# Attention output turned by VectorE in 32x32 blocks, self terms turned through DRAM, the tanh input taken from x W1 plus attention times (Wo W1), the loop written out

## The chip, the core and the metric

One core of a Trainium2 chip runs the program. The metric is the device time of one execution in microseconds. TensorE (PE) does the matrix products and can turn 128x128 tiles, VectorE (DVE), ScalarE (ACT) and GpSimd (POOL) work elementwise, and SyncE (SP) issues the transfers between DRAM and the on-chip memory. Each engine takes its instructions in order and waits on semaphores.

## The reference, cut to what matters

For 8 batches, x and side are 256 rows by 256 columns. There are 16 heads of 16 columns.

```python
# layer 0: attention of side's rows over x's keys and one own key ("self")
q = (side + b_self) @ Wq + bq
k_prev, k_self = (x + b_prev) @ Wk + bk, (side + b_self) @ Wk + bk
v_prev, v_self = x @ Wv + bv, side @ Wv + bv
score = concat([mask(q k_prev^T), sum(q * k_self)]) / 4      # per head
w = softmax(score)
attn = w[..., :-1] @ v_prev + w[..., -1:] * v_self
x1 = x + attn @ Wo + bo
# layer 1: pooling under a mask chosen by an integer per batch
s = tanh(x1 @ W1 + b1) @ v
out = x1 + softmax(masked(s)) @ x1 / count
```

## The kernel before

**Periods and slots.** The work is a pipeline over periods, numbered -1 to 9 here (`i` and `k` in the code: period 2i+k). In period n three or four batches are on the way: `nxt` is batch n+1 (its inputs are turned and q, k, v made), `b` is batch n (its score maxima are found), `prv` is batch n-1 (exponentials, product with v, normalization), `old` is batch n-2 (product with Wo, layer 1, output). Each period of TensorE has eight slots; each slot begins with one head pair's scores for the maximum (L1037) and one pair's scores for the exponential (L1050), which lags six slots, and then holds a piece of the other work. All periods are written in one function per engine; on the compute engines periods 3 to 6 run in a hardware loop of two periods per turn, the others are written out (SP's loop holds periods 2 to 5).

**Precision.** fp32 operands of large products are split into a rounded `hi` and a rest `lo`, and three products are summed: twelve TensorE instructions for a 256x256x256 product (L1010).

**Maxima.** VectorE reduces the scores of each pair (L798). There is one PSUM tile for these scores, so a slot's max scores wait for the maximum of the slot before. After four pairs the negated maxima are turned on TensorE (L1071; in slot 5 for the first half, in slot 0 of the next period for the second), copied by ScalarE and sent by SP into two rows of the q operand (L323), from which the exp scores take them.

**Attention output.** With v in 32-column groups, TensorE makes the output of four heads at a time with columns on partitions (L1063), ScalarE copies it to SBUF (`o_sb`, L519), TensorE turns it back (L1233, eight turns per batch, slot 7), VectorE adds the self term and its weight (L959, L963), GpSimd multiplies with the reciprocal sum (L469). In the next period TensorE turns `attn` again (L1142), ScalarE and VectorE split it into `at_hi` and `at_lo` (L567, L850), and TensorE makes the product with Wo (slot 2). VectorE adds `x_bo`, that is x plus the output bias, and so has x1. TensorE turns x1 (L1168), the two engines split that, and Z = x1 W1 follows in slot 4 with six products (L1188), then the tanh, then the product that spreads the score row over all partitions (L1202, tile SB).

**SP's queue.** In each period SP issues, in this order: loads of x and side two batches ahead, the second half's maxima, the spills of q and k parts to DRAM for the next batch (L305), the first half's maxima, the placing of the next batch's rows from DRAM (L314 and the mask L353, first half, then second half), and the load of `xr_sb`, x again in rows for the residual (L362). It waits for each piece's producers in this order.

**GpSimd's order.** The self product `vs_p` of `prv`, `q_lo`, the rest of x1 (L458), `attn` of `prv`, `x_bo` of `prv` (L479, waits for the load of `xr_sb`), then the issue of the output store of `old` (L484).

**Shared PSUM.** Four PSUM banks are handed from step to step by the table `SHARED`, whose entries name the bank and the reader that frees it.

## Time and profile before

| | us |
|---|---|
| median of three runs | 287.01 (286.06 to 287.28) |
| the profiled execution | 285.36, its span 283.7 |
| TensorE busy | 235.7 (83%) |
| VectorE busy | 174.6 (62%) |
| ScalarE busy | 150.1 (53%) |
| GpSimd busy | 65.6 (23%) |

The mean granted clock of TensorE was 0.937. A row of the timeline gives the start in us from the span's start, the duration, the engine, the source line, the operation with output and inputs, how many instructions are merged, and in brackets the idle time before it with what ended it. Rows of the windows view give the busy time of each engine in a stretch. TensorE's instructions overlap one another, so distances between starts say more than durations.

### The profile page before, as it was taken

Reading aid. Unit: us, or ns where it says so; the run is one execution under the profiler, and the core shown is the slowest. Engines: PE = TensorE matmul, PEld = TensorE weight load, DVE = VectorE, ACT = ScalarE, POOL = GpSimd, SP = SyncE. Lnnn points to the kernel's source line nnn. Section 1 sums busy time; section 2 is a strip of 40 time slices with the busy share of each in tenths; the row PEclk is TensorE's granted clock in tenths of the full one; section 3 lists DMA queues with packets and bytes.
Section 4 is the critical chain, followed back from the end, with each engine's and each line's share of the span. In section 5 each row is a group of like instructions: output and inputs, shape, how many; then the busy total and the mean of one; then the engine's idle time right before and its main releaser. Section 6 shows DMA issues by size and latency. Waiting matters only on the chain.

```text
span 283.7 us, 6002 instructions
## 1 busy us (share of the span) xinstructions
PE 235.7 (83%) x2084; PEld 186.7 (66%) x2084; DVE 174.6 (62%) x367; ACT 150.1 (53%) x289; POOL 65.6 (23%) x80
## 2 busy tenths in 40 slices
PE   2967598898899999999999999999998868666543
PEld 1866476677678777877887888688875636435422
DVE  2636665457568678758774978297748756324231
ACT  4341314474586657656865685468565656650220
POOL 8060010030151016101700270045005203404101
PEclk9999979599999999999999999799999999999555
DMA  6359866733964394359445943754375110201001
GB/s 151 101 191 246 162 210 160 158 112 117 206 154 166 101 206 165 130 137 228 143 138 127 211 152 111 172 94 148 111 170 101 37 39 1 77 0 39 0 0 37
DMA packets 28277, 35.50 MB, mean 125 GB/s; under 512 B 4440, under 2 KB 24672, under 8 KB 28256
## 3 DMA queue, kind: packets, MB, share of 16 engines
q1 hardware_dynamic: 27616, 33.12, 45.7%
q0 software_dynamic: 640, 2.10, 2.1%
q8 instruction: 13, 0.21, 0.3%
q14 instruction: 8, 0.07, 0.1%
HBM read 20.26 MB, written 14.69 MB: 123 GB/s over the span
## 4 chain that ended last, share of the span: by engine, by line
PE 57%; DMA 13%; DVE 11%; issue 9%; ACT 5%; SPq 3%; DVEq 0%; POOL 0%; ACTq 0%
PE ps_any L1010 20%; PE ps_any L1063 9%; DMA q_rows<-mt_sb 7%; PE ps_max L1037 7%; PE ps_any L1017 6%; PE ps_exp L1050 5%; DVE s_max L798 4%; DMA k_rows<-k_spill 3%; SPq L323 2%; PE ps_any L1188 2%; PE ps_any L1120 2%; PE ps_any L1233 2%; DMA x_sb<-in_x 2%; DVE o_out L983 1%; PE ps_max L1082 1%
## 5 line engine op out<-in xcount | busy, mean ns | idle before, releaser
L798 DVE TENSOR_REDUCE s_max<-ps_max 128x4 f32<-128x1024 f32 x64 | 78.0, 1219 | 26.0 <-PE ps_max L1037 25.7
L512 ACT ACTIVATE pt<-ps_exp 128x1024 f32<-128x1024 f32 x64 | 65.7, 1027 | 33.8 <-PE ps_exp L1050 33.5
L1037 PE MATMUL ps_max<-k_rows,q_rows 49*128 49x256 f32 x256 | 33.1, 338 | 9.5 <-DVE s_max L798 4.9
L469 POOL TENSOR_TENSOR attn<-num,rden 128x256 f32<-128x256 f32 x16 | 9.6, 621 | 124.4 <-DVE rden L968 124.4
L1063 PE MATMUL ps_any<-pt,v_aug 128*32 128x256 f32 x512 | 36.0, 401 | 1.3 <-DVE masked L924 1.3
L1037 PEld LDWEIGHTS ps_max<-k_rows,q_rows 49*128 49x128 f32 x256 | 19.8, 190 | 25.6 <-issue 13.8
L1050 PE MATMUL ps_exp<-q_rows,k_rows 51*128 51x256 f32 x256 | 27.9, 296 | 9.3 <-DMA q_rows<-mt_sb 8.3
L1050 PEld LDWEIGHTS ps_exp<-q_rows,k_rows 51*128 51x128 f32 x256 | 20.2, 190 | 13.3 <-DMA q_rows<-mt_sb 10.4
L1063 PEld LDWEIGHTS ps_any<-pt,v_aug 128*32 128x32 f32 x512 | 13.7, 112 | 12.8 <-issue 3.6
L1010 PE MATMUL ps_any<-st_hi,w_hi 128*128 128x256 f32 x64 | 20.7, 323 | 0.2 <-DVE st_lo L826 0.2
L1010 PE MATMUL ps_any<-st_hi,w_lo 128*128 128x256 f32 x64 | 19.1, 298 | 0.0
L1010 PE MATMUL ps_any<-st_lo,w_hi 128*128 128x256 f32 x64 | 19.1, 298 | 0.0
L942 DVE TENSOR_TENSOR pool_pt_lo<-ps_any,pool_pt_hi 128x512 fp32r<-128x512 f32 x8 | 5.5, 692 | 21.8 <-ACT pool_pt_hi L650 21.8
L434 POOL TENSOR_TENSOR q_lo<-q_full,q_hi 128x512 fp32r<-128x512 f32 x8 | 10.3, 1282 | 27.4 <-ACT q_hi L683 26.1
L519 ACT ACTIVATE o_sb<-ps_any 128x256 f32<-128x256 f32 x32 | 12.1, 379 | 7.9 <-PE ps_any L1063 7.7
L446 POOL TENSOR_TENSOR vs_p<-v_self,p_self 128x256 f32<-128x256 f32 x16 | 9.6, 620 | 23.6 <-ACT p_self L576 23.5
L1010 PEld LDWEIGHTS ps_any<-st_hi,w_hi 128*128 128x128 f32 x64 | 13.4, 209 | 1.6 <-DVE st_lo L826 0.6
L458 POOL TENSOR_TENSOR x_lo<-x,x_hi 128x512 fp32r<-128x512 f32 x8 | 10.2, 1274 | 15.5 <-ACT x_hi L585 15.5
L1010 PEld LDWEIGHTS ps_any<-st_hi,w_lo 128*128 128x128 f32 x64 | 13.3, 208 | 0.0
L895 DVE SCALAR_TENSOR_TENSOR k_lo<-ps_any,bqk_col,k_hi 128x256 fp32r<-128x256 f32 x16 | 7.0, 480 | 10.0 <-ACT k_hi L601 10.0
L1010 PEld LDWEIGHTS ps_any<-st_lo,w_hi 128*128 128x128 f32 x64 | 13.2, 206 | 0.0
L1010 PE MATMUL ps_any<-xt_hi,w_hi 128*128 128x256 f32 x32 | 10.7, 335 | 2.5 <-ACT q_hi L683 2.5
(141 smaller groups left out, 568.8 us busy)
## 6 DMA issues: line engine op xcount, KB each, us to landing
q_rows<-q_spill SPq DMA_DIRECT2D x32, 192.0 KB, 4.4
k_rows<-k_spill SPq DMA_DIRECT2D x32, 192.0 KB
q_spill<-q_hi SPq DMA_DIRECT2D x16, 256.0 KB, 2.5
k_spill<-k_hi SPq DMA_DIRECT2D x16, 256.0 KB, 2.5
s_sb<-in_fside_BxSxS SPq DMA_DIRECT2D x8, 256.0 KB, 6.1
x_sb<-in_x SPq DMA_DIRECT2D x8, 256.0 KB, 5.8
q_spill<-q_lo SPq DMA_DIRECT2D x8, 256.0 KB, 2.3
k_spill<-k_lo SPq DMA_DIRECT2D x8, 256.0 KB, 2.7
```

The source lines that it names most:

```text
L434: nc.gpsimd.tensor_tensor(lo[:], full[:], hi[:].bitcast(F32), ALU.subtract).then_inc(lo_done, 1)
L446: last = nc.gpsimd.tensor_tensor(vs_p[:, t].rearrange("p (h d) -> p h d", d=DH), v_self[:, par, t].rearrange("p (h d) -> p h d", d=DH), p_ ...
L458: nc.gpsimd.tensor_tensor(x1_lo[:], x1[:], x1_hi[:].bitcast(F32), ALU.subtract).then_inc(x1_lo_done, 1)
L469: nc.gpsimd.tensor_tensor(attn[:, t].rearrange("p (h d) -> p h d", d=DH), num[:, t].rearrange("p (h d) -> p h d", d=DH), rden[:, t].unsque ...
L512: nc.scalar.activation(pt[:, at:at + 2], ps_exp[:], ACT.Exp).then_inc(p_ready, 1)
L519: nc.scalar.activation(o_sb[:, g], ps_any[:, bank_free(f"PV{g}", i, k)[0], 0, :], ACT.Copy).then_inc(pv_copied, 1)
L798: nc.vector.tensor_reduce(s_max[:, j // MJ, :, j % MJ], ps_max[:], AX.X, ALU.max).then_inc(max_found, 1)
L1010: last = pe.matmul(out_of[:, m], lhs, rhs, start=(j == 0), stop=(j == len(terms) - 1))
L1017: last = pe.transpose(out_of[:, kb, P * t:P * t + P], src[:, t, P * kb:P * kb + P], ident[:])
L1037: last = pe.matmul(ps_max[:, e, t], q_rows[par][rows, j, P * t:P * t + P], k_rows[par][rows, j, :], start=True, stop=True)
L1050: last = pe.matmul(ps_exp[:, e, t], k_rows[par][rows, j, P * t:P * t + P], q_rows[par][rows, j, :], start=True, stop=True)
L1063: last = pe.matmul(bank[32 * c:32 * c + 32, 0, :], v_aug[par][:, t, h, :], pt[:, h % 8, t, :], start=(t == 0), stop=(t == KB - 1), skip_gr ...
```

## The change

1. **Attention output.** v's columns are put in another head order (by the way Wv is split), and four heads out of every fourth group share a step, so that VectorE can turn a PSUM bank of 128 x 512 in 32x32 blocks straight into rows (`turn`, twice per batch: after slot 3's maxima and after slot 7's). GpSimd adds the self terms (two instructions of 272 elements per partition) and multiplies with the reciprocals (two of 256), VectorE turns the result back with two 128x256 turns into `at_full`, ScalarE makes `at_hi` at the end of the period, and GpSimd makes `at_lo` as its first work of the next period. The `o_sb` copies, TensorE's turns of `o_sb` and `attn` and their PSUM banks go.
2. **Self terms.** GpSimd writes the weighted self values and their weights to `self_nat`; SP stores that to DRAM after the spills and loads it back in four transfers (`self_turned`, 128 x 544 bytes each) between the first half's maxima and the placing of the next batch's rows.
3. **tanh input.** Z is made from x turned (four buffers kept) times W1 plus attn turned times (Wo W1): twelve products in slot 3 instead of six in slot 4; x1 is no longer turned or split that way. (Wo W1) and its bias are made once in period 0. SB moves from slot 5 to slot 4.
4. **Head order of the score rows** (`slot_of`), with Wq and Wk split in two or four instructions where there were one or two, and the bias loads of q and k issued as eight transfers by ScalarE at the start instead of two by SP.
5. **Loop.** All eleven periods are written out on every engine.

```diff
 @@ sync, period @@
                 if live(*nxt):
                     spill(*nxt, (q_hi, q_lo), q_copied, q_lo_done, (0, 0, 1), q_spill, q_placed, 32, q_spilled)
                     spill(*nxt, (k_hi, k_lo), k_hi_done, k_lo_done, (0, 1, 0), k_spill, k_placed, 48, k_spilled)
+                if live(*prv):
+                    sp.wait_ge(vs_p_done, count(*prv, 1, 1))
+                    sp.dma_start(self_dram, self_nat[:].rearrange("p (c g) t d -> p c (g t d)", c=4)
+                                 ).then_inc(self_stored, 16)
                 if live(*b):
                     place_max(*b, 0)
+                if live(*prv):
+                    if (n := count(*prv, 2, 0)) is not None:
+                        sp.wait_ge(sum_done, n)
+                    sp.wait_ge(self_stored, count(*prv, 16, 16))
+                    for c in range(4):
+                        sp.dma_start(self_turned[32 * c:32 * c + 32].rearrange("p w n d -> p w (n d)"),
+                                     self_dram.rearrange("(w i) c m -> c i w m", i=32)[c]
+                                     ).then_inc(self_placed, 16)
 @@ gpsimd, period @@
+                if live(*old):
+                    pool.wait_ge(at_hi_done, count(*old, 1, 1))
...
+                    nc.gpsimd.tensor_tensor(at_lo[:], at_full[:], at_hi[:].bitcast(F32), ALU.subtract
+                                            ).then_inc(at_lo_done, 1)
                 if live(*prv):
...
-                    for t in range(KB):
-                        last = nc.gpsimd.tensor_tensor(
...
+                    nc.gpsimd.tensor_tensor(
+                        self_nat[:, :, :, 0:DH],
+                        v_self[:, par].rearrange("p t (n d) -> p n t d", d=DH),
+                        self_nat[:, :, :, DH:DH + 1].broadcast_to([P, H, KB, DH]), ALU.mult
+                        ).then_inc(vs_p_done, 1)
...
                 if live(*prv):
-                    pool.wait_ge(rden_done, count(*prv, 1, 1))
-                    for t in range(KB):
-                        pool.wait_ge(num_done, count(*prv, 2, t + 1))
-                        nc.gpsimd.tensor_tensor(
-                            attn[:, t].rearrange("p (h d) -> p h d", d=DH),
...
+                    pool.wait_ge(self_placed, count(*prv, 64, 64))
+                    for a in range(2):
+                        half = slice(NG * a, NG * a + NG)
+                        pool.wait_ge(o_turned_done, count(*prv, 2, a + 1))
+                        nc.gpsimd.tensor_tensor(
+                            o_turned[:, half, :, 0:DH + 1], o_turned[:, half, :, 0:DH + 1],
+                            self_turned[:].rearrange("p w n d -> p n w d")[:, half], ALU.add).then_inc(sum_done, 1)
...
+                    for a in range(2):
+                        pool.wait_ge(rden_done, count(*prv, 2, a + 1))
+                        nc.gpsimd.tensor_tensor(
+                            attn[:, a].rearrange("p n b d -> p b n d"),
...
+                                ).broadcast_to([P, 2, 8, DH]), ALU.mult).then_inc(attn_done, 1)
 
                     pool.wait_ge(xr_loaded, count(*prv, 16, 16))
 @@ scalar, period @@
-            def pv_copy(i, k, g):
...
-                nc.scalar.activation(o_sb[:, g], ps_any[:, bank_free(f"PV{g}", i, k)[0], 0, :], ACT.Copy).then_inc(pv_copied, 1)
                 exp_slot(3)
                 if live(*old):
-                    act.wait_ge(x1t_ready, count(*old, 1, 1))
-                    nc.scalar.activation(x1t_hi[:], ps_any[:, bank_free("X1T", i, k)[0]], ACT.Copy
-                                         ).then_inc(x1t_hi_done, 1)
+                    act.wait_ge(z_ready, count(*old, 1, 1))
...
+                    nc.scalar.activation(z_sb[0:A], ps_any[0:A, bank_free("Z", i, k)[0], 0, :], ACT.Tanh,
+                                         bias=b1_full[:, 0:1]).then_inc(tanh_done, 1)
...
                 exp_slot(7)
                 if live(*nxt):
...
+                if live(*prv):
+                    act.wait_ge(at_full_done, count(*prv, 2, 2))
...
+                    nc.scalar.activation(at_hi[:], at_full[:], ACT.Copy).then_inc(at_hi_done, 1)
...
+                for n, vec in enumerate((bq, bk)):
+                    for e, odd in ((0, 0), (0, 1), (1, 0), (1, 1)):
+                        act.dma_start(bqk_raw[odd::2, n, e:e + 1], vec.rearrange("(m e b d) -> e b d m", e=2, b=2, d=DH)[e, odd]
+                                      ).then_inc(bias_loaded, 16)
             weight_hi(0)
 @@ vector @@
+            def turn(i, k, a, pi, pk):
+                dve.wait_ge(pv_ready, count(i, k, NG, 2 * a + 2))
...
+                nc.vector.transpose(o_turned[:, NG * a:NG * a + NG].rearrange("p n w d -> p (n w d)"),
+                                    ps_any[:, bank_free("PVAB"[0:2] + "AB"[a], pi, pk)[0]].rearrange("p b q -> p (b q)")
+                                    ).then_inc(o_turned_done, 1)
...
                 if live(*b):
                     max_of(*b, 3)
                     group_max(*b, 0)
+                if live(*prv):
+                    turn(*prv, 0, i, k)
...
                     max_of(*b, 7)
                     group_max(*b, 1)
                 if live(*prv):
-                    natural = [ps_any[:, bank_free(f"NAT{t}", i, k)[0]].rearrange("p t (h c) -> p (t h) c", c=32)
-                               for t in range(KB)]
...
+                    turn(*prv, 1, i, k)
+                    for a in range(2):
+                        dve.wait_ge(sum_done, count(*prv, 2, a + 1))
+                        nc.vector.reciprocal(rden[:, half], o_turned[:, half, :, DH]).then_inc(rden_done, 1)
+                    for a in range(2):
+                        dve.wait_ge(attn_done, count(*prv, 2, a + 1))
+                        nc.vector.transpose(at_full[:, a], attn[:, a].rearrange("p n b d -> p (n b d)")
+                                            ).then_inc(at_full_done, 1)
...
+                if (i, k) == (0, 0):
+                    dve.wait_ge(w1o_ready, 1)
+                    nc.vector.tensor_copy(w1o_hi[:], ps_any[:, 3, :, 0:A]).then_inc(w1o_hi_done, 1)
+                    nc.vector.tensor_tensor(bias_col[:], ps_any[:, 3, :, A], bo_col[:], ALU.add
+                                            ).then_inc(bias_col_done, 1)
...
                 if live(*b):
                     max_of(*b, 5)
 @@ tensor, period @@
                 score_slot(3)
-                if live(*old):
-                    bank = take_bank("X1T", i, k)
-                    pe.wait_ge(x1_done, count(*old, 1, 1))
-                    transposed(bank, x1).then_inc(x1t_ready, 1)
                 if live(*nxt):
-                    products(bank, xt_hi, xt_lo, 1, True).then_inc(k_ready, 1)
+                    products(bank, *xt, 1, True).then_inc(k_ready, 1)
                 if live(*old):
                     bank = take_bank("Z", i, k)
-                             for w, x in ((w1_hi, x1t_hi), (w1_lo, x1t_hi), (w1_hi, x1t_lo))]
+                    terms = [(kb, w, x) for (w_a, w_b), (x_a, x_b) in (((w1_hi, w1_lo), old_xt),
+                                                                     ((w1o_hi, w1o_lo), (at_hi, at_lo)))
+                             for kb in range(KB) for w, x in ((w_a, x_a), (w_b, x_a), (w_a, x_b))]
+                if (i, k) == (0, 0):
+                    pe.wait_ge(wo_turned_done, 1)
...
+                                pe.matmul(ps_any[:, 3, kb, 0:A], wo_turned[:, nb, P * kb:P * kb + P], w1[:, nb, :],
+                                          start=(nb == 0), stop=(nb == KB - 1))
...
+                                last = pe.matmul(ps_any[:, 3, m, A:A + 1], w_raw[:, 3, kb, P * m:P * m + P],
+                                                 bv_col[:, kb:kb + 1], start=(kb == 0), stop=(kb == KB - 1))
 
                 score_slot(4)
...
+                if live(*old):
+                    bank = take_bank("SB", i, k)
+                    pe.wait_ge(tanh_done, count(*old, 1, 1))
                 score_slot(6)
-                    products(v_bank, xt_hi, xt_lo, 2, False, (0,))
...
                 score_slot(7)
                 if live(*nxt):
-                    products(v_bank, xt_hi, xt_lo, 2, False, (1,)).then_inc(v_ready, 1)
...
-                        for gg in range(NG):
-                            last = pe.transpose(bank[:, gg // 2, P * (gg % 2):P * (gg % 2) + P],
-                                                o_sb[:, gg, P * t:P * t + P], ident[:])
+                    products(bank, *xt, 2, False).then_inc(v_ready, 1)
```

## Rows read from the trace of the kernel before

**Rows 1.** Windows, period 4: us, busy us (instructions) PE PEld DVE ACT POOL, PEclk, DMA share, GB/s
```profile
131.70:158.79 27.09, 26.33 (x260) 21.37 (x259) 20.25 (x42) 17.91 (x35) 6.95 (x8) 1.00 0.59 154
```

**Rows 2.** Timeline of TensorE, single lines: start us, us, engine, line, operation, count, idle before
```profile
66.83 0.28 PE L1071 MATMUL ps_any<-ident,neg_max 128*32 128x128 f32 x1
...
148.04 0.28 PE L1071 MATMUL ps_any<-ident,neg_max 128*32 128x128 f32 x1
...
151.99 0.50 PE L1050 MATMUL ps_exp<-q_rows,k_rows 51*128 51x256 f32 x4 [0.57 <-DMA q_rows<-mt_sb]
...
158.79 0.51 PE L1037 MATMUL ps_max<-k_rows,q_rows 49*128 49x256 f32 x4
...
161.20 0.50 PE L1037 MATMUL ps_max<-k_rows,q_rows 49*128 49x256 f32 x4
...
164.98 0.39 PE L1010 MATMUL ps_any<-w_hi,at_hi 128*128 128x256 f32 x1
...
174.93 0.28 PE L1071 MATMUL ps_any<-ident,neg_max 128*32 128x128 f32 x1
...
203.51 0.28 PE L1071 MATMUL ps_any<-ident,neg_max 128*32 128x128 f32 x1
...
219.93 0.36 PE L1010 MATMUL ps_any<-w_hi,at_hi 128*128 128x256 f32 x1 [0.52 <-DVE at_lo L850]
...
228.30 0.28 PE L1071 MATMUL ps_any<-ident,neg_max 128*32 128x128 f32 x1
```

**Rows 3.** Chain that ended last, in order of time: start us, us, what
```profile
145.74 0.70 PE ps_any L1188 x6
...
156.57 0.87 PE ps_any L1233 x8
```

**Rows 4.** Timeline of GpSimd, early in periods 5 and 7
```profile
159.17 1.20 POOL L469 TENSOR_TENSOR attn<-num,rden 128x256 f32<-128x256 f32 x2 [16.64 <-DVE rden L968]
...
162.61 1.30 POOL L479 TENSOR_TENSOR x_bo<-xr_sb,bias_out 128x512 f32<-128x512 f32 x1 [2.23 <-DMA xr_sb<-in_x]
...
163.85 0.75 POOL L484 DMA_DIRECT2D out<-o_out  x1
...
166.22 1.29 POOL L434 TENSOR_TENSOR q_lo<-q_full,q_hi 128x512 fp32r<-128x512 f32 x1 [0.40 <-ACT q_hi L683]
...
217.27 1.27 POOL L479 TENSOR_TENSOR x_bo<-xr_sb,bias_out 128x512 f32<-128x512 f32 x1 [1.45 <-DMA xr_sb<-in_x]
```

**Rows 5.** Timeline of SP's queue, period 4, placing the next batch's rows
```profile
150.82 0.80 SPq L314 DMA_DIRECT2D q_rows<-q_spill  x2
...
152.47 0.91 SPq L314 DMA_DIRECT2D k_rows<-k_spill  x2
```

**Rows 6.** Windows, the busy DMA stretch at the end of period 4, columns as in rows 1
```profile
152.00:161.00 9.00, 9.00 (x93) 6.95 (x93) 5.99 (x16) 4.65 (x8) 1.20 (x2) 1.00 0.98 192
```

**Rows 7.** Timeline of VectorE, end of period 4 and start of period 5
```profile
158.00 0.18 DVE L813 SCALAR_TENSOR_TENSOR neg_max<-t_max,neg_max 128x16 fp32r<-128x16 f32 x1
...
159.15 0.86 DVE L983 SCALAR_TENSOR_TENSOR o_out<-ps_any,pool_r,x 128x256 f32<-128x256 f32 x2
...
159.93 1.22 DVE L798 TENSOR_REDUCE s_max<-ps_max 128x4 f32<-128x1024 f32 x1
...
163.52 0.69 DVE L846 TENSOR_TENSOR xt_lo<-ps_any,xt_hi 128x512 fp32r<-128x512 f32 x1 [0.19 <-ACT xt_hi L561]
```

**Rows 8.** Timeline of the head: ScalarE, SP's queue, VectorE
```profile
0.88 1.28 ACT L530 ACT_TABLE_LOAD   x1 [0.88 <-PEq L1267]
...
4.54 1.19 ACT L530 ACTIVATE w_hi<-w_raw 128x256 fp32r<-128x256 f32 x2 [2.38 <-DMA w_raw<-in_L_cond_Wq]
...
4.66 0.59 SPq L377 DMA_DIRECT2D bqk_raw<-in_L_cond_bk  x1
...
5.22 1.81 DVE L708 SCALAR_TENSOR_TENSOR w_lo<-w_raw,w_hi 128x128 fp32r<-128x128 f32 x4 [5.22 <-ACT w_hi L530]
```

**Rows 9.** Timeline of VectorE, period 0
```profile
41.47 0.87 DVE L910 SCALAR_TENSOR_TENSOR prod<-ps_any,bqk_col,q_full 128x256 f32<-128x256 f32 x2
```

More of the change, by code:

```diff
@@ L391, in _ @@
             sp.dma_start(mask_dram, mask_row[:]).then_inc(masks_stored, 16)
-            for i, k in BEFORE_DMA:
-                period(i, k)
-            with sp.Fori(LOOP_FROM, LOOP_TO) as i:
-                for k in BODY_DMA:
-                    period(i, k)
-            for i, k in AFTER_DMA:
+            for i, k in PERIODS:
                 period(i, k)
@@ L988, in _ @@
             weight_lo(0)
-            for i, k in BEFORE:
-                period(i, k)
-            with dve.Fori(LOOP_FROM, LOOP_TO) as i:
-                for k in BODY:
-                    period(i, k)
-            for i, k in AFTER:
+            for i, k in PERIODS:
                 period(i, k)
@@ L1060, in pv @@
                 for t in range(KB):
-                    for c in range(GRP):
-                        h = GRP * g + c
-                        last = pe.matmul(bank[32 * c:32 * c + 32, 0, :], v_aug[par][:, t, h, :],
-                                         pt[:, h % 8, t, :], start=(t == 0), stop=(t == KB - 1),
+                    for c in range(4):
+                        last = pe.matmul(bank[32 * c:32 * c + 32, g % 2, :], v_aug[par][:, t, NG * c + g, :],
+                                         pt[:, 4 * (g % 2) + c, t, :], start=(t == 0), stop=(t == KB - 1),
                                          skip_group_check=True)
@@ L1122, in pooled @@
                     return last
+                xt = [half[(2 * i + k + 1) % 4] for half in (xt_hi, xt_lo)]
                 score_slot(0)
@@ L1245, in _ @@
             pe.wait_ge(ident_ready, 1)
-            for i, k in BEFORE:
-                period(i, k)
-            with pe.Fori(LOOP_FROM, LOOP_TO) as i:
-                for k in BODY:
-                    period(i, k)
-            for i, k in AFTER:
+            for i, k in PERIODS:
                 period(i, k)
```

313 lines of the change are left out of this document (155 added, 158 removed), and 9 rows, old and new, of the table SHARED.

## The prediction

> **What bounds the kernel now.** I read the table of busy time by period first. In period 4 TensorE is busy 26.33 of 27.09 us and every other engine at most 20.3 [rows 1]; the granted clock is 1.00 there, the upper of its two levels. So the middle of the run is TensorE's list of work, written out in slots, and a change there is worth what it takes off that list minus the waits that it makes. Next I read TensorE in order of time. I measure from "MT0", the transpose of the negated maxima in slot 5, because from it hang the placing of the maxima, then the placing of the next batch's rows, then the load of xr, all on SP's queue. From MT0 of period 4 (148.04) to that of period 5 (174.93) it is 26.89 us; from period 1 (66.83) to period 6 (203.51) five intervals take 136.68 [rows 2]. Within one: the exp scores of slot 6 wait for the placed maxima and start at MT0+3.95; the next period starts at +10.75; its second max scores at +13.16; the product with Wo at +16.94; from there 9.95 to the next MT0 [rows 2]. There are few gaps in this, so several other chains could be nearly as late; these are what the change must be held against.
>
> **What comes off TensorE.** Eight transposes of o_sb cost 0.87 us [rows 3]; the four of attn and the four of x1, of the same shape, half of that each, 0.43. Against them stand six more products in Z, six of which cost 0.70 [rows 3]. Sum: -1.03 us per period. The score-row product (SB) moves from behind MT0 to before it: 0.25 us out of the stretch MT0 to slot 6, which buys nothing, as that stretch ends with the wait for the placed maxima, and 0.25 into the stretch before MT0. The four o_sb copies and two splits that ScalarE and VectorE lose lie on engines with 7 to 9 us to spare per period [rows 1], so I give them nothing.
>
> **What the new path costs, and who stands behind it.**
>
> *SP.* Four loads of self_turned stand between the placed maxima and the rows of the next batch. Two issues of row placement take 0.80 to 0.91 us [rows 5]; four take 1.83. The bytes, 0.28 MB, go at the 192 GB/s of the busy stretch [rows 6] in 1.45 us, inside that time and while the DMA engines would be waiting for the first rows; they stay at 0.98 busy for nine microseconds after it [rows 6], so nothing downstream catches up. All that follows in the queue (rows, xr, x, side) lands 1.83 later, bounds 1.45 (bytes alone) and 3.3 (both in turn). The store of self_nat lies before MT0 in a stretch with free DMA time: 0.
>
> *GpSimd.* Here lies the cost that I think decides. x_bo waits for the xr load: it starts at 162.61 after 2.23 us of waiting, MT0+14.57; the one after period 6 starts at 217.27, 13.76 behind that period's MT0 [rows 2, 4]. I take 14.2. Before, only x1 needed it, and at_lo was VectorE's. Now at_lo is GpSimd's and stands first in the next period, so behind x_bo and behind the issue of the output store, and the Wo product waits for it. Its time: MT0 + 14.2 + 1.83 (SP) + 1.30 (x_bo) + 0.75 (store issue) + 1.29 (at_lo, priced as q_lo) [rows 4] + 0.1 = 19.47, against 16.94 before. From Wo to the next MT0: 9.95 - 0.43 + 0.70 + 0.25 = 10.47. The interval becomes 29.94. Five of them less 0.75 (period 1 stores no output) are 148.95 against 136.68: **+12.3**. Queued behind the late at_lo are self_nat's product and q_lo, whose spills SP sends in order; both had room of some microseconds. Bounds of this term: below, no wait, -1.03 per interval, -5.2; above, with SP's 3.3, +19.6.
>
> *VectorE at the period's end.* The turn of a 128x512 bank is not in this trace. The nearest row is the 128x512 subtraction out of PSUM, 0.69 us [rows 7]; half that for 128x256. Bounds: 0.35 (half) to 1.22 (the 128x1024 reduction [rows 7]). The Trainium skill (Vector Engine (DVE) Microarchitecture Reference, "The reshape front-end and per-opcode configuration") says that the transposing mode sustains one element per cycle per lane; with the 0.96 GHz of its VectorE page (VectorE: DVE Perf Modes, "Specifications") that is an estimate of 0.53 us and a start-up. By it the turn would be cheaper by up to 0.15, and no run here shows it yet. The group maximum ended at MT0+10.14 [rows 2, 7]; about 0.85 earlier now, since half of V stood before slot 7: +9.3. Then turn 0.69, GpSimd's sum of 272 elements 0.65, two scalings 1.20 [rows 4], the last turn back 0.35, four handovers 0.4, output 0.86, the first maximum 1.22 [rows 7]: MT0+14.67. TensorE's second max scores stood at +13.16 and would now be ready at 12.3. A stall of 2.4 us, but it ends before at_lo does, so it is inside the 19.47 and counts only if at_lo is early.
>
> *The Wo product of period 7* waits alike: 13.76 + 1.83 + 3.34 + 0.1 = 19.03 against 16.42 [rows 2]: **+2.6**. From there to period 7's MT0 it took 8.37 [rows 2]; without the x1 transposes, their two splits and the wait for them about 7.5: **-0.9**.
>
> *Head.* ScalarE first issues eight bias DMAs. SP took 0.59 for one such [rows 8]; bounds 0.4 and 0.7. Eight are 4.7 from 0.9 on; if the table load of 1.28 comes after them it ends at 6.9, where Wq's first split began at 4.54 [rows 8]; that split is now four instructions instead of two, and VectorE's eight instead of four (1.81 for four [rows 8]). Q waits for it. I take **+2.5**, bounds 0.5 and 4.
>
> *Period 0.* w1 times Wo and the bias products, about 1.3 us, stand before slot 4's scores, and VectorE's three instructions on them follow the 0.87 us product for the self scores [rows 9], with slot 5 waiting on them: **+2.4**, bounds 0 and 3.5.
>
> *Periods 8 and 9* have no scores to cover anything. They lose the attn and x1 turns, each 0.43 and a 0.69 split on VectorE [rows 3, 7] with one on ScalarE beside it, at least 2.2 us, and the o_sb turns; they gain the round trip above (turn, sum, scalings, turn back: 3.3 us), x_bo and the store issue ahead of at_lo, and the longer Z. I take 0, bounds -3 and +3.
>
> *Loops.* The interval from period 4 to 5 crosses the loop's back edge and takes 26.89, the mean of five is 27.34 [rows 2]: the edge costs nothing to see, and writing the periods out 0.
>
> **Sum.** 12.3 + 2.6 - 0.9 + 2.5 + 2.4 = +18.9. The profiled execution took 285.36 us (span 283.7), so 304.3; the three runs have a median of 287.01, 0.6% above it. I predict 304.
>
> **Rivals.**
> (a) *The late load is not the stop*: SP's four loads cost less queue time than I think, or xr comes through, and VectorE's round trip is what remains. Interval 14.67 + (174.93 - 161.20 = 13.73) - 0.86 + 0.70 + 0.25 = 28.5 [rows 2]; five are 142.5, +5.8; period 7 +0.6; head and period 0 +4.9: 296.7. For it: x_bo's distance from MT0 already differs by 0.8 us between the two periods shown. Against: in both GpSimd was idle for xr [rows 4], and rival (a) needs it more than 3 us earlier than I have it.
> (b) *Only the start is longer*: TensorE's saving cancels the stalls. 285.4 + 4.9 = 290.
> (c) *The other side, faster*: the shorter list of TensorE counts. Place: slots 0 to 2 of each period. Price: -1.03 in six periods, -6, with the head's DMAs hidden behind the weights: 279. It decides only if at_lo is done by MT0+16 and the maximum of slot 0 by MT0+12.3. For it: before, TensorE was the only full engine [rows 1]. Against: at_lo would have to be ready before xr itself lets x_bo end (14.2 + 1.83 + 1.30).
> (d) *More than the sum*: the loads of self_turned cost bytes and issue in turn, 1.5 us more in each of six periods: 313.
>
> **How the numbers follow.** Main case 0.55, (a) 0.20, (b) 0.08, (c) 0.12, (d) 0.05. About half a percent, 1.4 us, is what a measurement of this kernel can tell from no change. Faster is (c), 0.12; slower is the main case, (a), (d) and nearly all of (b), 0.85; no change is the rest, 0.03. A range from 290 to 312 leaves out (c) and most of (d).
>
> **What would show it.** The changed kernel's timeline should have the Wo product of periods 2 to 7 waiting for GpSimd's at_lo, and x_bo before it waiting for xr some 16 us after MT0; the second max scores waiting for VectorE some 2 us; intervals between MT0s of 29 to 30 us; TensorE busy for about 25.3 us of each; the turn near 0.7 us; the first split of Wq starting near 7 instead of 4.54. If at_lo is ready early and the intervals are under 27, the prediction is wrong at its main step; if ScalarE's DMA issues are short, at its head.

## The result and the profile after

| | before | after |
|---|---|---|
| median of four runs, us | 286.53 (285.50 to 287.28) | 330.39 (327.38 to 334.69) |
| profiled execution, its span | 285.36, 283.7 | 331.58, 329.7 |
| TensorE busy | 235.7 (83%) | 255.8 (78%) |
| TensorE idle | 48.0 | 73.9 |
| mean granted clock | 0.937 | 0.839 |

The changed kernel is slower: ratio 1.150, 95% interval 1.139 to 1.160. I had the direction, and a time of 304. Some executions of one kernel come out slower at a lower clock; ratios here and below leave them out, medians do not, so steps between kernels are compared by their ratios to the kernel before, run on the same chip.

The cadence between two MT0s comes first, as it did before [rows 2]. Single lines of TensorE's timeline after (start us, us, engine, line, operation, count, idle before):

```profile
72.85 0.28 PE L1094 MATMUL ps_any<-ident,neg_max 128*32 128x128 f32 x1
...
136.99 0.28 PE L1094 MATMUL ps_any<-ident,neg_max 128*32 128x128 f32 x1 [2.20 <-DVE masked L957]
...
151.83 1.11 PE L1040 MATMUL ps_any<-ident,s_sb 128*128 128x128 f32 x4 [2.44 <-DVE o_out L1011]
152.88 1.94 PE L1086 MATMUL ps_any<-pt,v_aug 128*32 128x256 f32 x16
...
158.22 0.39 PE L1033 MATMUL ps_any<-w_hi,at_hi 128*128 128x256 f32 x1
...
171.15 0.28 PE L1094 MATMUL ps_any<-ident,neg_max 128*32 128x128 f32 x1 [2.20 <-DVE masked L957]
...
239.47 0.29 PE L1094 MATMUL ps_any<-ident,neg_max 128*32 128x128 f32 x1 [2.20 <-DVE masked L957]
...
271.83 0.28 PE L1094 MATMUL ps_any<-ident,neg_max 128*32 128x128 f32 x1 [2.19 <-DVE masked L957]
```

From period 1 (72.85) to period 6 (239.47) five intervals take 166.6 us, 29.9 more than before, where I forecast 12.3. The next interval is 7.6 longer (forecast 1.7), the stretch up to 72.85 is 6.0 longer (4.9), and what follows 271.83 is 2.5 longer (0). Together these are the 46.0 us by which the span grew, so most of the miss lies in the cadence.

The interval from 136.99 is 34.16 us; from period 4 to 5 it was 26.89 [rows 2]. The product with Wo (158.22) waits for nothing; it is late because two things ahead of it wait, MT0 for VectorE's `masked` and the transpose of side for VectorE's `o_out`. The windows of the same interval (us, busy us (instructions) PE PEld DVE ACT POOL, PEclk, DMA share, GB/s), the whole and its parts but for the first 0.95 us:

```profile
137.00:171.15 34.15, 29.51 (x248) 22.78 (x249) 21.58 (x40) 16.53 (x30) 9.57 (x10) 0.85 0.53 142
137.95:144.70 6.75, 6.75 (x45) 4.90 (x43) 1.60 (x2) 2.44 (x7) 0.74 (x1) 0.50 0.58 144
144.70:149.38 4.68, 4.68 (x42) 4.09 (x41) 3.17 (x8) 2.23 (x3) 0.73 (x2) 0.99 1.02 196
149.38:151.83 2.45, 0.01 (x1) 0.00 (x0) 1.95 (x6) 0.78 (x2) 1.16 (x3) 0.95 1.10 265
151.83:155.00 3.17, 3.17 (x22) 1.57 (x24) 2.47 (x3) 1.51 (x3) 3.10 (x3) 0.50 0.37 134
155.00:171.15 16.15, 13.95 (x138) 11.27 (x139) 12.00 (x22) 8.94 (x15) 3.85 (x4) 1.00 0.35 117
```

TensorE is idle for 34.15 - 29.51 = 4.64 us, which is the two waits. It is busy for 29.51 where the same work takes 25.32 at a clock of 1.00 (window of e3 below): 4.2 us more, because behind each of the two waits stands a stretch, 6.75 and 3.17 us long, in which the granted clock is 0.50, the 1.2 GHz level. Against the 27.09 of [rows 1], with 26.33 busy, the interval is 7.1 longer: 1.0 less work, 4.2 of slower clock, 3.9 more idle. Over the five intervals, before and after:

```profile
66.83:203.51 136.68, 131.03 (x1274) 105.43 (x1272) 98.65 (x192) 87.98 (x170) 34.17 (x39) 0.99 0.59 153
```

```profile
72.85:239.47 166.62, 141.29 (x1226) 109.25 (x1224) 104.09 (x191) 82.18 (x146) 47.22 (x49) 0.88 0.53 143
```

TensorE's idle time grows from 5.7 to 25.3 us and its busy time by 10.3, although the list is shorter. TensorE's waits over the whole run (us in total, times, longest us):

```profile
PE ps_any L1094 <- DVE masked L957: 13.2, 6, 2.2
PE ps_any L1040 <- DVE o_out L1011: 8.7, 4, 2.5
...
PE ps_any L1033 <- POOL at_lo L453: 4.6, 1, 4.6
```

Neither of the first two was in the prediction; the third was its main term, and it occurs once, in period 9. VectorE's timeline shows what stands behind them:

```profile
134.60 1.22 DVE L813 TENSOR_REDUCE s_max<-ps_max 128x4 f32<-128x1024 f32 x1
135.74 0.41 DVE L957 TENSOR_TENSOR masked<-hidden,ps_any 128x256 f32<-128x256 f32 x1
...
136.53 0.41 DVE L957 TENSOR_TENSOR masked<-hidden,ps_any 128x256 f32<-128x256 f32 x1
...
147.77 0.17 DVE L828 SCALAR_TENSOR_TENSOR neg_max<-t_max,neg_max 128x16 fp32r<-128x16 f32 x1
147.86 0.71 DVE L837 STREAM_TRANSPOSE o_turned<-ps_any 128x512 f32<-128x512 f32 x1
...
150.00 1.02 DVE L995 STREAM_TRANSPOSE at_full<-attn 128x256 f32<-128x256 f32 x2 [0.32 <-POOL attn L490]
150.94 0.83 DVE L1011 SCALAR_TENSOR_TENSOR o_out<-ps_any,pool_r,x 128x256 f32<-128x256 f32 x2
151.69 1.22 DVE L813 TENSOR_REDUCE s_max<-ps_max 128x4 f32<-128x1024 f32 x1
```

The second `masked` ends at 136.94 (136.53 + 0.41) and MT0 starts at 136.99; `o_out` ends at 151.77 (150.94 + 0.83) and the transpose of side starts at 151.83. Each pair shares a PSUM bank in the new table `SHARED`: SB (which `masked` reads) and MT0 have bank 0, PO (which `o_out` reads) and TS, the transpose of side, have bank 2.

### The profile page after: what moved, and what is told of

It is laid out like the page before. It is cut to its first block, busy times and chain, and to the rows that moved or that the text cites. A ratio compares the mean times of both kernels' runs of the same rounds, so it can differ in the third digit from the quotient of the medians.

```text
span 329.7 us, 5553 instructions
## 1 busy us (share of the span) xinstructions
PE 255.8 (78%) x2028; PEld 199.9 (61%) x2028; DVE 180.1 (55%) x367; ACT 139.0 (42%) x254; POOL 86.6 (26%) x96
## 4 chain that ended last, share of the span: by engine, by line
PE 59%; DVE 13%; issue 10%; DMA 5%; ACT 5%; POOL 3%; SPq 2%; ACTq 2%; DVEq 0%; POOLq 0%
PE ps_any L1033 21%; PE ps_any L1086 12%; PE ps_max L1060 7%; PE ps_any L1040 6%; DVE s_max L813 4%; PE ps_exp L1073 4%; PE ps_any L1204 4%; PE ps_any L1115 2%; POOL attn L490 2%; DMA q_rows<-mt_sb 2%; DVE masked L957 2%; ACTq L696 2%; DVE o_turned L837 1%; DVE o_out L1011 1%; DMA k_rows<-k_spill 1%
## 5 line engine op out<-in xcount | busy, mean ns | idle before, releaser
L1060 PE MATMUL ps_max<-k_rows,q_rows 49*128 49x256 f32 x256 | 36.2, 364 | 14.6 <-DVE s_max L813 7.4
L482 POOL TENSOR_TENSOR o_turned<-o_turned,self_turned 128x272 f32<-128x272 f32 x16 | 11.8, 736 | 132.7 <-DMA self_turned<-self_dram 94.9
L1086 PE MATMUL ps_any<-pt,v_aug 128*32 128x256 f32 x512 | 44.8, 480 | 1.1 <-ACT pt L529 1.1
L1060 PEld LDWEIGHTS ps_max<-k_rows,q_rows 49*128 49x128 f32 x256 | 22.1, 213 | 33.2 <-issue 18.9
L1073 PEld LDWEIGHTS ps_exp<-q_rows,k_rows 51*128 51x128 f32 x256 | 22.8, 215 | 10.6 <-DMA q_rows<-mt_sb 6.8
L445 POOL TENSOR_TENSOR q_lo<-q_full,q_hi 128x512 fp32r<-128x512 f32 x8 | 10.3, 1284 | 32.7 <-ACT q_hi L689 27.6
L1040 PE MATMUL ps_any<-ident,s_sb 128*128 128x128 f32 x32 | 8.3, 410 | 12.3 <-DVE o_out L1011 8.7
L460 POOL TENSOR_TENSOR self_nat<-v_self,self_nat 128x512 f32<-128x512 f32 x8 | 8.9, 1108 | 31.8 <-ACT self_nat L582 31.8
L671 ACT ACTIVATE at_hi<-at_full 128x512 fp32r<-128x512 f32 x8 | 5.1, 632 | 27.3 <-DVE at_full L995 27.3
L1033 PEld LDWEIGHTS ps_any<-st_hi,w_hi 128*128 128x128 f32 x64 | 13.5, 211 | 4.6 <-DVE st_lo L850 3.7
L1033 PE MATMUL ps_any<-w_hi,at_hi 128*128 128x256 f32 x32 | 11.6, 363 | 4.6 <-POOL at_lo L453 4.6
L891 DVE TENSOR_TENSOR x<-ps_any,x_bo 128x512 f32<-128x512 f32 x8 | 5.5, 692 | 17.7 <-PE ps_any L1033 17.7
L472 POOL TENSOR_TENSOR x_lo<-x,x_hi 128x512 fp32r<-128x512 f32 x8 | 10.3, 1285 | 18.4 <-ACT x_hi L596 18.4
```

The source lines that it names most:

```text
L445: nc.gpsimd.tensor_tensor(lo[:], full[:], hi[:].bitcast(F32), ALU.subtract).then_inc(lo_done, 1)
L460: nc.gpsimd.tensor_tensor(self_nat[:, :, :, 0:DH], v_self[:, par].rearrange("p t (n d) -> p n t d", d=DH), self_nat[:, :, :, DH:DH + 1].br ...
L472: nc.gpsimd.tensor_tensor(x1_lo[:], x1[:], x1_hi[:].bitcast(F32), ALU.subtract).then_inc(x1_lo_done, 1)
L482: nc.gpsimd.tensor_tensor(o_turned[:, half, :, 0:DH + 1], o_turned[:, half, :, 0:DH + 1], self_turned[:].rearrange("p w n d -> p n w d")[: ...
L1033: last = pe.matmul(out_of[:, m], lhs, rhs, start=(j == 0), stop=(j == len(terms) - 1))
L1040: last = pe.transpose(out_of[:, kb, P * t:P * t + P], src[:, t, P * kb:P * kb + P], ident[:])
```

## The experiments

All kernels are the changed one with small edits, each built on the last unless it says otherwise; e4 and e8 are edits of the kernel before.

**e1 and e2: one bank each.**

```diff
 e1
-    ("V", 1, 1, ("v_copied", 1)), ("PO", -2, 2, ("out_done", 1)),
+    ("V", 1, 2, ("v_copied", 1)), ("PO", -2, 1, ("out_done", 1)),
 e2 (without e1)
-    ("MT0", 0, 0, ("mt_copied", 1)),
+    ("MT0", 0, 1, ("mt_copied", 1)),
```

> The changed kernel with the PSUM banks of V and PO exchanged (V in bank 2, PO in bank 1), so that the turn of side (TS, bank 2) no longer waits for VectorE's output of the batch before last. Theory A (two PSUM handovers hold TensorE, and each hold is followed by a stretch at 1.2 GHz): the wait of 2.45 us before TS goes, but slot 1's max scores then wait for VectorE's first maximum (16.0 us after the maxima's transpose, now 17.75): interval 34.2 -> 32.4, total 319 to 322. Theory B (my forecast: the late load of x and at_lo behind it set the interval): no change, 330.

Measured: median 323.78, ratio 1.120 (1.111 to 1.130), 3.0 points or 8.6 us less, a little less than A had. That this is about the 8.7 of the wait is chance. The wait for `o_out` is gone, but TensorE now waits there for the first maximum of a period, 11.4 us where it was 7.4 in the changed kernel, and 7.1 for at_lo where it was 4.6; its idle time does not fall at all, and what was won is time at the slow clock (table behind e4):

```profile
PE ps_max L1060 <- DVE s_max L813: 11.4, 10, 2.1
```

> The changed kernel with the transposed maxima MT0 in bank 1 instead of bank 0, which the spread score row SB holds until VectorE's second masked add. Theory A: the wait of 2.20 us goes in six periods, and with it the 6.8 us at 1.2 GHz behind it (3.4 us each): -5.6 per period, total about 297. If the clock falls for another reason, only the wait goes: 317. Theory B: at_lo cannot be ready before about 18.3 us after MT0, interval not under 29.0, total 299.

Measured: median 316.36, ratio 1.096 (1.086 to 1.106). The wait of MT0 is gone with 5.4% of the kernel before's time, some 15 us. In the profiled executions 11.3 of the 15.8 us are idle time, out of the wait's 13.2, and 4.5 are busy time, the slow clock. My 297 was wrong: I had counted all of the slow clock behind the wait to it.

**e3: both.**

> Both bank exchanges. Theory A with VectorE's round trip next in line: interval 28.5, no stretch at 1.2 GHz in the middle of the run, total about 295 to 297. Theory B: the Wo product waits for at_lo behind x_bo, interval 29.5 to 30, total 301 to 304 (what I forecast for the change as a whole). Either way slower than the kernel before (287).

Measured: median 314.11, ratio 1.085 (1.075 to 1.096). The two handovers are 6.5 of the 15.0% together; 8.5% stay. Both answers (295 to 297, and 301 to 304) are missed: more stands behind the handovers than either had, and the slow clock is not gone. An interval without a slow stretch (columns as above):

```profile
164.29:193.37 29.08, 25.32 (x251) 20.20 (x250) 21.31 (x40) 16.33 (x30) 9.51 (x10) 1.00 0.59 167
```

TensorE's work is 25.32 us, 1.0 under [rows 1] as predicted, but there are 3.76 us of idle in it.

**e4: the kernel before with the shared bank alone.** SB moved to the end of slot 4 there, into MT0's bank:

```diff
-    ... ("MT0", 0, 0, ("mt_copied", 1)), ("SB", -2, 2, ("masked_done", 2)),
+    ... ("SB", -2, 0, ("masked_done", 2)), ("MT0", 0, 0, ("mt_copied", 1)),
```

> The kernel before with one piece of the change: the spread score row SB is made at the end of slot 4 and in bank 0, the bank of MT0 behind it. Theory A: TensorE waits some 2.2 us for VectorE's masked adds in each of six periods, and the clock falls to 1.2 GHz behind each: +5.6 per period, total 315 to 322. If the clock does not follow the wait: +13, total 300. If the wait is covered: 287.

Measured: median 310.98, ratio 1.083 (1.076 to 1.090). One handover between two small pieces of work costs the old kernel 24 us, between the 300 of a clock that does not follow the wait and the 315 of one that falls every time. The wait and two intervals:

```profile
PE ps_any L1071 <- DVE masked L924: 13.5, 6, 2.3
```

```profile
159.19:188.44 29.25, 26.59 (x258) 21.29 (x259) 20.13 (x41) 17.97 (x35) 6.95 (x8) 1.00 0.53 146
188.44:221.49 33.05, 30.78 (x259) 24.71 (x259) 20.31 (x41) 18.18 (x35) 6.90 (x8) 0.85 0.46 113
```

Both begin right behind the same wait of 2.27 us. The first keeps a clock of 1.00 and is 2.36 longer than [rows 2] has it; the second runs at 0.85 and is 3.8 longer still. So the wait is paid every time and the slow clock in some intervals; what decides which ones is not shown. The profiled executions so far (us; idle is span less busy):

| | span | TensorE busy | idle | mean clock |
|---|---|---|---|---|
| before | 283.7 | 235.7 | 48.0 | 0.937 |
| after | 329.7 | 255.8 | 73.9 | 0.839 |
| e1 | 320.8 | 243.9 | 76.9 | 0.861 |
| e2 | 313.9 | 251.3 | 62.6 | 0.852 |
| e3 | 311.1 | 244.5 | 66.6 | 0.877 |
| e4 | 310.3 | 251.9 | 58.4 | 0.881 |

Of what the shared bank adds to the kernel before in e4, 10.4 us are idle time and 16.2 the same work at a slower clock.

**e12: my main term alone, in the changed kernel.** x_bo behind at_lo on GpSimd, nothing else:

```diff
                     nc.gpsimd.tensor_tensor(at_lo[:], at_full[:], at_hi[:].bitcast(F32), ALU.subtract
                                             ).then_inc(at_lo_done, 1)
+                    pool.wait_ge(xr_loaded, count(*old, 16, 16))
...
+                    nc.gpsimd.tensor_tensor(x_bo[:], xr_sb[:], ...).then_inc(x_bo_done, 1)
```

> The changed kernel with x_bo behind the next period's at_lo on GpSimd, and nothing else: my forecast's main term by itself. By the forecast (Wo gated by at_lo, 29.9 us a period against 27.1): some 12 us off 330, 318. By the trace of the changed kernel (Wo starts 3 us behind at_lo there, the two banks gate): 328 to 332.

Measured: median 331.83, ratio 1.158 (1.140 to 1.177): nothing. GpSimd's and TensorE's timelines:

```profile
184.97 0.75 POOL L506 DMA_DIRECT2D out<-o_out  x1 [1.53 <-DVE o_out L1011]
185.74 1.28 POOL L453 TENSOR_TENSOR at_lo<-at_full,at_hi 128x512 fp32r<-128x512 f32 x1
```

```profile
191.03 0.39 PE L1033 MATMUL ps_any<-w_hi,at_hi 128*128 128x256 f32 x1
```

at_lo is ready at 187.0 and its reader comes 4 us later.

**e5 and e6: the same term with the handovers out of the way.** e5 is e3 with VectorE's turn back (L995) moved from in front of `o_out` to behind the next period's first maximum, and ScalarE's `at_hi` behind `st_hi`; e6 adds the edit of e12.

```diff
 vector, e5
                 if live(*b):
                     max_of(*b, 0)
+                if live(*old):
+                    for a in range(2):
...
+                        nc.vector.transpose(at_full[:, a], ...).then_inc(at_full_done, 1)
```

> The kernel of e3 with VectorE's turn back of the attention output moved behind the next period's first maximum, and ScalarE's rounding of it behind side^T. e3 took 314.1 us; in a period without a slow clock its max-score matmuls lie 29.1 us apart, with 1.2 us of TensorE's idle in front of the second one of a period, behind VectorE's turn, rden, turn back and o_out (3.8 us between two maxima). Theory C (VectorE's round trip sets e3's period): five to six periods lose 1.0 to 1.2 us, 307 to 309 us. Theory B (my forecast: at_lo behind x_bo behind the late x rows): Wo can't start earlier than 18.4 us behind MT0, the gap only moves to Wo, 313 to 315 us.

Measured: median 308.57, ratio 1.087 (1.070 to 1.103). The median looks like theory C; the ratio, which counts, is e3's 1.085 within its interval. TensorE's waits say what happened, first e3's two rows, then e5's:

```profile
PE ps_max L1060 <- DVE s_max L813: 12.0, 12, 1.8
...
PE ps_any L1033 <- POOL at_lo L453: 6.4, 3, 4.6
```

```profile
PE ps_any L1034 <- POOL at_lo L453: 11.4, 8, 4.3
...
PE ps_max L1061 <- DVE s_max L813: 5.4, 7, 1.3
```

VectorE's wait falls by 6.6 us and the wait for at_lo grows by 5.0, as theory B said: the two were tied.

> The kernel of e5 with GpSimd's x_bo moved behind the next period's at_lo, so that at_lo no longer stands behind the late x rows. Theory C alone: nothing, as e5 within 1 us. Theory B: the period falls to what its TensorE work and the max rows' transfer leave (25.3 + about 1.9 of idle), 27.2 us, from e3's 29.1: 301 to 304 us if e5 stayed at 314. Both at once (C and B tie in e3): e5 little, this one 301 to 304.

Measured: median 301.75, ratio 1.056 (1.040 to 1.072), 3.1 points under e5. The wait for at_lo is down to one, outside the cadence:

```profile
PE ps_any L1034 <- POOL at_lo L453: 3.8, 1, 3.8
```

So x_bo ahead of at_lo, behind the late x rows, is a cost of the change, some 9 us once the turn back is late too; it was hidden by larger ones. The edit on e3 alone was not run.

**e7: the head.** The eight bias loads on SyncE's queue behind b_prev; Wo's transpose, its copy and the product with W1 at the end of period -1.

```diff
-                        act.dma_start(bqk_raw[odd::2, n, e:e + 1],
+                        sp.dma_start(bqk_raw[odd::2, n, e:e + 1],
...
-                if (i, k) == (0, 0):
+                if first:
                     transposed(ps_any[:, 3], w_raw[:, 3]).then_inc(wo_turned_ready, 1)
```

> The kernel of e6 with the eight bias loads on SyncE's queue behind b_prev, as in the kernel before, and the product W1^T Wo^T with Wo's transpose at the end of period -1 in place of period 0. If the longer head is these two (MT0 of period 0 at 49.2 us in e3 against 42.05 before: 2.4 of ScalarE's issues, 4.5 in period 0): 5 to 6 us off e6. If period 0 is longer for its slow clock alone: 2.4 off.

Measured: median 297.41, ratio 1.033 (1.014 to 1.051): 2.3 points, some 6.5 us; the intervals of e6 and e7 overlap.

**e8: the loops alone.**

```diff
-            for i, k in BEFORE:
-                period(i, k)
-            with pe.Fori(LOOP_FROM, LOOP_TO) as i:
...
+            for i, k in PERIODS:
+                period(i, k)
```

> The kernel before with its four loops written out and nothing else changed. All theories: 287, within 1.5 us of the kernel before. If fetching more instructions costs anything, as no trace so far shows, it is over 290.

Measured: median 289.06, ratio 1.004 (0.994 to 1.013): nothing to see.

**e9: the maxima earlier.** MT0 and ScalarE's copy of it from behind slot 5 into slot 4, ahead of SB.

```diff
-    ... ("SB", -2, 0, ("masked_done", 2)), ("PVB", -1, 3, ("o_turned", 2)),
-    ("MT0", 0, 1, ("mt_copied", 1)),
+    ... ("MT0", 0, 0, ("mt_copied", 1)), ("PVB", -1, 3, ("o_turned", 2)),
+    ("SB", -2, 0, ("masked_done", 2)),
```

> The kernel of e7 (297.4 us) with MT0 and ScalarE's copy of it moved from behind slot 5 to behind the KS product in slot 4, in bank 0, and SB behind PVB. In e7 TensorE waits 0.97 us in every period for the max rows' transfer, 3.9 us behind MT0, the place that SB left free when it moved ahead of MT0. If that move is what costs the 0.97: seven periods, 290 to 292 us. If what gates is the row placing behind SyncE's self loads: the wait moves there, 296 to 298.

Measured: median 289.97, ratio 1.014 (1.002 to 1.027), as expected of the first theory; the intervals of e7 and e9 overlap, but TensorE's wait for the max rows' transfer falls from 13.5 us in ten to 4.4 in three. Behind it the next wait shows, at the first maximum of the next period. The profile names nothing that ended it ("issue"); that it is for rows that SyncE places is what e13 tests:

```profile
PE ps_max L1060 <- issue: 13.7, 6, 4.1
```

**e10 and e11: the self loads on GpSimd.** e10 is e7 with the four loads of `self_turned` issued by GpSimd; e11 is e9 with that, and VectorE's split of the product W1^T Wo^T at the end of period -1.

```diff
-                        sp.dma_start(self_turned[32 * c:32 * c + 32].rearrange("p w n d -> p w (n d)"),
+                        pool.dma_start(self_turned[32 * c:32 * c + 32].rearrange("p w n d -> p w (n d)"),
```

> The kernel of e7 with the four loads of the turned self terms issued by GpSimd, which is idle there, in place of SyncE. SyncE's 1.77 us go, its row placing and the x rows start that much earlier. In e7 TensorE waits at the next period's first or second maximum for rows (0.9 to 1.1 us in two periods, 3.1 in one). If SyncE's issues are the cause: 293 to 295 us. If not (the DMA queues or VectorE set it): 297.

Measured: median 297.70, ratio 1.042 (1.030 to 1.055): no gain over e7.

> e9 and e10 together, and VectorE's split of W1^T Wo^T at the end of period -1, which takes 1.6 us of TensorE's wait out of period 0. If the costs of the change are the handovers and queue places found so far: 283 to 288 us, level with the kernel before (287) or a little under. If something else costs as well: 290 to 293.

Measured: median 303.32, ratio 1.062 (1.051 to 1.072). Much worse than e9, which I did not expect. GpSimd's timeline in e11, and VectorE's waits there:

```profile
161.97 2.22 POOL L487 DMA_DIRECT2D self_turned<-self_dram  x4 [9.33 <-DMA self_dram<-self_nat]
170.73 1.41 POOL L494 TENSOR_TENSOR o_turned<-o_turned,self_turned 128x272 f32<-128x272 f32 x2 [6.54 <-DMA self_turned<-self_dram]
```

```profile
DVE rden L986 <- POOL o_turned L494: 27.5, 14, 4.9
```

The loads are issued in time (2.22 us for four) and the sum still waits 6.54 us behind the last issue. VectorE waits for the sum with the next period's first maximum behind it. SyncE issues the row placing from 160.63 to 165.40 there, so that the two compete is likely; it was not tried apart.

**e13 and e14: the self loads on SyncE, later.** e13 is e9 with SyncE's wait for the stored self terms and the four loads between the two halves of the row placing; e14 adds VectorE's split at the end of period -1.

```diff
                         place(k_spill, k_rows[par], k_placed, g)
+                        if g == 0:
+                            load_self()
```

> The kernel of e9 (290.0 us) with SyncE's wait for the stored self terms and their four loads moved from ahead of the row placing to between its two halves. In e9 TensorE waits 1.1 to 4.1 us in every period (13.7 in six) at the next period's first maximum, for rows whose placing starts 2.7 us late on SyncE: 0.96 of waiting for the store, 1.76 of issues. If SyncE's place for the loads is the cause: 1.3 to 2.2 us a period, 279 to 284 us, faster than the kernel before (287). If the transfers themselves set it (spill to landing), 289 to 291; if the self terms then come too late to the sum, as with GpSimd's loads in e11, over 295.

Measured: median 280.19, ratio 0.988 (0.980 to 0.995), as expected if SyncE's place for the loads is the cause. The 13.7 us of "issue" are gone; the wait for VectorE's maxima rises from 5.4 to 15.0.

> The kernel of e13 with VectorE's split of W1^T Wo^T at the end of period -1, nothing else. Its 2.2 us of TensorE's wait in period 0 (by the trace of e9) go: e13 less 1.5 to 2.2 us. If period 0 waits for VectorE's maxima anyway: e13 within 1 us.

Measured: median 278.33, ratio 0.981 (0.972 to 0.990): faster than both kernels. One interval, five intervals, the largest wait that TensorE has left, and a wait of VectorE:

```profile
144.27:171.20 26.93, 25.35 (x251) 20.20 (x248) 20.24 (x41) 16.29 (x31) 9.49 (x10) 1.00 0.65 180
65.08:197.73 132.65, 124.24 (x1224) 98.87 (x1222) 97.80 (x187) 79.95 (x145) 46.80 (x49) 1.00 0.66 176
```

```profile
PE ps_max L1064 <- DVE s_max L818: 15.1, 11, 2.0
```

```profile
DVE rden L993 <- POOL o_turned L501: 10.1, 14, 2.0
```

In ratio points the way from 1.150 to 0.981 is: the two handovers 6.5, x_bo with the turn back 3.0, the head 2.3, the maxima's place 1.8, the self loads' place 2.7, the split 0.65.

**e15: the kernel before with e9's order.** e14 is 1.9% under the kernel before, but e9's order is no part of the change. So the kernel before got the same move of MT0 alone; there Z goes behind the third product with v, and VS, the product for the self values, ahead of SB:

```diff
-    ... ("Z", -2, 0, ("tanh_done", 1)), ("PV2", -1, 3, ("pv_copied", 3)),
-    ("MT0", 0, 0, ("mt_copied", 1)), ("SB", -2, 2, ("masked_done", 2)), ("VS", 1, 1, ("vs_copied", 1)),
+    ... ("MT0", 0, 0, ("mt_copied", 1)), ("PV2", -1, 3, ("pv_copied", 3)),
+    ("Z", -2, 0, ("tanh_done", 1)), ("VS", 1, 1, ("vs_copied", 1)), ("SB", -2, 2, ("masked_done", 2)),
```

> The kernel before with the edit of e9 alone: MT0 and ScalarE's copy of it in slot 4, behind KS, and Z behind the third product with v. e14 is 1.9% faster than the kernel before; is that the changed arithmetic (1.0 us less of TensorE's work in a period) or the reordering that came on the way? In the kernel before TensorE is idle 0.6 to 1.2 us in an interval, of which the maxima's transfer ends about 0.6. If the gain is the reordering's: 279 to 282 us (ratio 0.98). If it is the shorter list: 285 to 288 (ratio 0.995 to 1.005).

Measured: median 273.74, ratio 0.948 (0.939 to 0.957), the fastest of all and better than I gave either answer. One interval of it and five, all at the upper level of the clock:

```profile
140.41:166.73 26.32, 26.31 (x261) 21.35 (x258) 20.11 (x41) 17.83 (x35) 6.94 (x8) 1.00 0.61 162
62.79:193.20 130.41, 128.54 (x1268) 103.92 (x1266) 97.71 (x192) 87.86 (x169) 33.93 (x39) 1.00 0.59 158
```

TensorE has no gap in the one interval and takes 26.32 us; e14 has 1.0 us less work but 1.58 us of waits for VectorE's maxima, and takes 26.93. Over five intervals e14 has 4.3 us less work and 6.5 more idle. So e14's lead over the kernel before needs no changed arithmetic: about the same reordering alone gives more. In the form of e14 the changed arithmetic gives nothing back. Its shorter list is used up by VectorE's longer chain, which waits 10.1 us for GpSimd's sums, a wait that the kernel before does not have, ahead of the maxima that TensorE waits for. Whether yet another order would free the shorter list was not tried.

## Why the prediction was wrong

**The step that failed** is the sentence on SB: "0.25 us out of the stretch MT0 to slot 6, which buys nothing". I priced the move by its length on TensorE, not by the bank it uses. In the kernel before, SB stood behind MT0 in a bank of its own; the change puts it right ahead of MT0 in MT0's bank, so MT0 waits for SB, for VectorE's maximum ahead of `masked` (134.60), and for both `masked`: 2.20 us, six times. e2 takes it out for 5.4 points, e4 puts it into the kernel before for 8.3. The table with the banks, whose lines the edits of e1, e2 and e4 show, is part of the change; I read it for the order and not for who frees what.

**VectorE at the period's end** was nearly right in length and wrong in place. I had the first maximum ready at MT0+14.67, hence `o_out` at MT0+13.45; it ended at MT0+14.78. The round trip from the end of the group maximum to `o_out` took 3.83, less than my 4.15; it began 1.65 late, at MT0+10.95 for my 9.3, with the 6.75 us of slow clock in between. I held a stall of 2.4 in front of the second max scores to be hidden under at_lo's 19.47. The stall of 2.44 that came is another, and the like size is chance: since PO now lies in the bank of TS, TensorE waits for `o_out` ahead of everything up to Wo, so Wo moves too (MT0+21.2) and nothing hides it. This second handover was not in the prediction either.

**The slow clock** was not in the sum at all. The row of period 4 had 1.00 [rows 1], and I let it stand for a list with 2 us holes in it. It is 4.2 of the 7.1 us of the interval shown. Over the five intervals TensorE is busy for 141.3 us with a list that e14 does in 124.2 at a clock of 1.00, so some 17 us of their 166.6 are the slow clock; the kernel before, at 0.99 there, has little of it. e3's and e4's intervals without a slow stretch show what is left when it stays away.

**GpSimd, the main term.** The chain is as I worked it out: x_bo waits for the x rows until MT0+14.9 (16.0 forecast), then store issue, then at_lo:

```profile
151.88 1.28 POOL L501 TENSOR_TENSOR x_bo<-xr_sb,bias_out 128x512 f32<-128x512 f32 x1 [1.34 <-DMA xr_sb<-in_x]
153.10 0.75 POOL L506 DMA_DIRECT2D out<-o_out  x1
153.87 1.29 POOL L453 TENSOR_TENSOR at_lo<-at_full,at_hi 128x512 fp32r<-128x512 f32 x1
```

at_lo is ready at MT0+18.2, 1.3 us before my 19.47, and three before Wo. So as a reason for the changed kernel's time it is wrong (e12: nothing), and as a cost of the change it is right (e6: 3.1 points, with the turn back late), below two that I had not seen. e3's interval of 29.08 beside my 29.94 is chance: there TensorE waits for VectorE (12.0 us over the run), the maxima's transfer (10.0), "issue" (6.5) and at_lo (6.4), and the four are nearly tied.

**SP's 1.83** was right in size:

```profile
138.97 1.77 SPq L352 DMA_DIRECT2D self_turned<-self_dram  x4
```

I said that nothing downstream catches up, and carried that to xr only. The rows themselves, placed late, were the last thing that kept the new order from gaining (e13: 2.7 points).

**Head and period 0.** ScalarE at the start:

```profile
0.75 2.59 ACTq L696 DMA_DIRECT2D bqk_raw<-in_L_cond_bq  x4
3.37 2.55 ACTq L696 DMA_DIRECT2D bqk_raw<-in_L_cond_bk  x4
5.95 1.28 ACT L537 ACT_TABLE_LOAD   x1 [5.95 <-issue]
7.25 1.34 ACT L537 ACTIVATE w_hi<-w_raw 128x128 fp32r<-128x128 f32 x4
```

The eight issues took 5.1 us for my 4.7. Wq's first split at 7.25 instead of 4.54 [rows 8], and 2.2 us on the start of period 0 (29.40 to 31.6): the head's 2.5 holds. Period 0 up to its MT0 took 4.5 us more (17.1 against 12.6), not 2.4. Moving the issues and the products together won 2.3 points, some 6.5 us (e7), for the 4.9 forecast. The wait in the row below is the part that I had seen (e14: 0.65 points); the rest I have not taken apart:

```profile
48.06 0.36 PE L1238 MATMUL ps_any<-bias_col,w 128*64 128x1 f32 x4 [1.58 <-DVE w1o_lo L941]
```

**Right:** TensorE's list (25.32 for 26.33), the turn out of PSUM (0.71 for 0.69), the loops (e8), periods 8 and 9 (2.5 us longer, inside the 3). By their means over the run the turns take 0.708 us for 512 columns and 0.445 for 256, which makes 1.03 ns an element and a start-up of 0.18, if reading from PSUM (512) and from SBUF (256) cost the same. The Trainium skill (Vector Engine (DVE) Microarchitecture Reference, "The reshape front-end and per-opcode configuration") has one element per cycle per lane, with which the trace agrees (1.04 ns at the prediction's 0.96 GHz). With the start-up, nothing is left of the 0.15 us by which the prediction thought the turn might be cheaper.

**The rivals.** (a) named VectorE's round trip, and was near its length; the bank put it in another place. (c) priced the shorter list at 279, and e14 takes 278.3, but e15 shows that this is not the list's doing: (c) fails too.

## What to carry to other kernels

When an edit moves a step in an order written out by hand, price it by the resource that it now shares with its neighbours, not by its length: ask of each step which bank it takes, who last read that bank, and what stands ahead of that reader on its engine. On an engine that was 97% busy a hole of 2 us can cost more than 2 us, because slow-clock stretches came with the holes here. And where several chains are nearly tied, mending one shows nothing (e5, e12) until its neighbours are mended too; and before a mended change is called a gain, give the old kernel the same mending (e15).

## What the hardware showed that I had not expected

The granted clock fell to 0.50, the 1.2 GHz level, behind stalls of TensorE of 2.2 to 2.5 us in a period that was otherwise full, for 6.75 and 3.17 us in the interval shown: 0.95 us after TensorE went on behind the first stall, and at once behind the second. In e4 the same stall of 2.27 us was followed by such a stretch in one interval and not in another. The Trainium skill (TensorE: Matmul & The Clock Gate, "A second HAM failure mode: psum-queue depth-cycling") tells of a kernel that hands PSUM banks round with small idle times and whose clock swings between the two levels. The trace agrees in part: the changed kernel's clock swings too, but behind one or two waits of over 2 us in an interval, and e4's interval at 1.00 shows that it need not.

The loads of `self_turned`, 68 KB each, took 2.0 us from issue to landing (median) when SyncE issued them in e9, and 5.3 when GpSimd did in e11, where SyncE was issuing the row placing at the same time; issuing four took 1.76 and 2.22 us.
